# Norm and gate products of expert choice inside the last periods of logic attention; LSTM choices of 24 steps laid singly over steps 1 to 3

## The chip, the cores and the metric

The kernel runs on one core of one Trainium2 chip. Its engines are PE (TensorE), DVE (VectorE), ACT (ScalarE), POOL (GpSimd) and SP (SyncE, which here only issues DMAs). Each engine runs its own list of instructions in order; they meet at semaphores. The metric is the device time of one execution in microseconds, as the median of several runs. Of the kernel before, three runs were timed.

## The reference, cut to what matters

The input is a batch of 32 images and 32 texts. A token stage makes 36 tokens of 128 features from each image and appends 77 text rows, so `h` holds 32 blocks of 113 x 128. Four layers follow, each added to its input:

```python
h = h + _L0_attn_ref(_layernorm(h), ...)   # logic attention: 8 heads, two score maps, a small convolution of six maps
h = h + _L0_ffn_ref(_layernorm(h), ...)    # expert choice: 8 experts each choose their 28 best rows of an image
h = h + _L1_attn_ref(_layernorm(h), ...)   # attention with relative places
h = h + _L1_ffn_ref(_layernorm(h), ...)    # 8 LSTM experts, 2 chosen for each row
```

Expert choice starts from the softmax of `x @ Wg` over the 8 experts, `x` being the layernormed rows. The last layer takes the 32 images as 32 time steps of 113 rows. For each row the two largest of 8 router logits are chosen (ties go to the lower expert) and weighted by a softmax of the two. Each of the 16 pairs (choice, expert) runs an LSTM over the steps on the rows masked with that choice:

```python
i_, f_, g_, o_ = split(xt @ Wi + h @ Wh + b)
c = sigmoid(f_) * c + sigmoid(i_) * tanh(g_)
h = sigmoid(o_) * tanh(c)
y = h @ Wo + bo
```

The output is the sum over the 16 pairs of mask times weight times `y`.

## The kernel before, in words

`build` keeps `h` (113 rows x 32 images x 128) and `hT` (128 x 32 x 113, the normed rows turned) in SBUF and calls four stages, each a `Phase` with its own tiles and semaphores that closes with a barrier of all engines. Inside a phase each `block()` closes with a barrier too.

**Logic attention** (`logic_attention`, lines 396 to 997) is a software pipeline over periods p = -4 to 33. In period p, image p goes through the convolution and its gates, image p-1 (m) has its scores mixed and raised to the exponential, image p-2 (e) is turned, attended, projected out and added to `h`, and images p+2 to p+4 (f, z) are prepared. The order is written out by hand for each engine. ACT switches between two tables of functions in every period (lines 809 and 822): one holds the gelu, the other the logarithm and the exponential. From period 30 on stages drop out: period 32 has only the mixing of image 31 and the output of image 30, period 33 only the output of image 31. In period 32 DVE does the mixing of image 31 before it copies the turned weights of image 30 (line 920); ACT raises the mix (763) between them.

**Expert choice** (`expert_choice`, from line 1000) has three blocks. The first only issues six DMAs on SP: the gate weights and five constants, w1 and w2 of 1 MB and b2 of 0.5 MB among them (lines 1018 to 1023). The second is `norm_and_turn` (lines 112 to 200), in four groups of eight images: DVE takes the row statistics, ACT the root, ACT and DVE scale the rows into `hn`, PE turns four images into one PSUM bank, ACT moves the bank to `hT`, and PE makes the gate products of the bank's images. The third block is the stage itself. Its DVE part makes the softmax of the gates. Its PE part begins with

```python
pe.wait_ge(consts_in, 80)
pe.wait_ge(s["gate_ready"], 1)
```

where 80 is all five constants, and then turns the gates (line 1100) for the choice of the 28 best rows.

**LSTM experts** (`lstm_experts`, from line 1583) runs the same norm for its router logits and then one block. Step t has 8 experts, n = 8t+e, and four pairs of experts, q = 4t+p. PE makes for each n four gates: three passes of the input (line 1749) and, from step 1, three of the state (1757), since float32 values are split into a high and a low float16 part. After expert 3 of step t it makes the output product of step t-1 (`outputs`, 1711) with the bias row (1712). ACT takes four gates per n (1794), the tanh of the cell (1801) and the high part of the state (1805). DVE's round q is: state of q-1 (1878), masked inputs of step t+1 (1867), low part of the state (1893), weighing (1886), the sum over the two choices (1900), then the new cell of q (a product 1907 and a sum 1910). The PSUM ring lets PE be three n ahead of ACT.

The choices of steps 0 to 7 are made before the first step. The choices of the other three groups of 8 steps are made in steps 1, 2 and 3 (`choice`, 7 and 6 small DVE operations, and `weigh_choices`, 3). PE turns each group's masks and weights behind expert 1 of the next step, ACT copies them, and SP writes them to DRAM. From there `masks(t)` and `weights(t)` load a step's masks, weights and weight rows (1681) spread over 128 partitions. `hT` is split into high and low parts in groups of 2, 6, 8, 8 and 8 images (`PARTS_OF`). The weights of the recurrent product are split in step 0, a pair in each round.

## Time and profile before

| what | us |
|---|---|
| timed runs | 2380.01, 2381.17, 2381.90 |
| median | 2381.17 |
| the profiled execution, own time | 2382.08 |
| its span | 2380.3 |
| PE busy | 2126.8 (89%) |
| DVE busy | 1712.8 (72%) |
| ACT busy | 1664.8 (70%) |
| POOL busy | 334.2 (14%) |
| mean granted clock of PE | 0.932 |

The profile is that of one execution. A timeline row has the start in us from the span's start, the duration, the engine, the source line, the operation, what it writes and reads, and how many such instructions in a row were merged (x8). In brackets stands the idle time of that engine just before, and what ended it. A stage row has the length of the stretch, then for PE, its weight loads (PEld), DVE, ACT and POOL the busy time and the instructions, then the granted clock (1.00 is 2.4 GHz, 0.50 is 1.2 GHz), the share of the DMA engines and GB/s. Busy time is summed over a stretch, and idle time of an engine that is not the bound costs nothing.

### The profile page before, as it was taken

Reading aid. Unit: us, or ns where it says so; the run is one execution under the profiler, and the core shown is the slowest. Engines: PE = TensorE matmul, PEld = TensorE weight load, DVE = VectorE, ACT = ScalarE, POOL = GpSimd, SP = SyncE. Lnnn points to the kernel's source line nnn. Section 1 sums busy time; section 2 is a strip of 40 time slices with the busy share of each in tenths; the row PEclk is TensorE's granted clock in tenths of the full one; section 3 lists DMA queues with packets and bytes.
Section 4 is the critical chain, followed back from the end, with each engine's and each line's share of the span. In section 5 each row is a group of like instructions: output and inputs, shape, how many; then the busy total and the mean of one; then the engine's idle time right before and its main releaser. Section 6 shows DMA issues by size and latency. Waiting matters only on the chain. (4 is left out here: it accounts for less than half of the span.)

```text
span 2380.3 us, 55433 instructions
## 1 busy us (share of the span) xinstructions
PE 2126.8 (89%) x22214; PEld 1520.6 (64%) x22214; DVE 1712.8 (72%) x2729; ACT 1664.8 (70%) x3075; POOL 334.2 (14%) x198
## 2 busy tenths in 40 slices
PE   6699999999999999998549799987789999999998
PEld 3554444544444444443137588846689999999997
DVE  4457888888888888886554344535898888888887
ACT  3478888888888888888523336732667777777776
POOL 0122222222222222221000013410000000000000
PEclk9589999999999999999759869997799999999998
DMA  6288888888888888888110000001212222122220
GB/s 181 69 246 225 235 230 221 227 227 228 234 227 220 230 225 233 230 228 202 45 45 1 10 2 2 2 24 72 83 61 69 75 75 70 65 72 70 75 75 21
DMA packets 113273, 305.20 MB, mean 128 GB/s; under 512 B 20559, under 2 KB 57545, under 8 KB 112506
## 3 DMA queue, kind: packets, MB, share of 16 engines
q1 hardware_dynamic: 113018, 301.66, 45.0%
q8 instruction: 177, 2.90, 0.5%
q14 instruction: 78, 0.64, 0.1%
HBM read 168.64 MB, written 80.65 MB: 105 GB/s over the span
## 5 line engine op out<-in xcount | busy, mean ns | idle before, releaser
L746 ACT ACTIVATE la_hid<-ps,la_b 128x904 f32<-128x904 f32 (+1 forms) x480 | 451.0, 991 | 105.1 <-PE ps L598 104.4
L1749 PE MATMUL ps<-ls_xm,ls_w_in_parts 128*128 128x226 f16 x3072 | 471.7, 263 | 10.5 <-DVE ls_xm L1867 5.2
L1757 PE MATMUL ps<-ls_state_parts,ls_w_rec_parts 128*128 128x226 f16 x2976 | 450.3, 260 | 0.0
L1794 ACT ACTIVATE ls_gates<-ps,ls_bias 128x226 f32<-128x226 f32 x768 | 299.3, 444 | 62.4 <-PE ps L1757 61.9
L1749 PEld LDWEIGHTS ps<-ls_xm,ls_w_in_parts 128*128 128x128 f16 x3072 | 296.6, 98 | 21.6 <-DVE ls_xm L1867 5.6
L598 PE MATMUL ps<-la_pairs,la_w 32*64 32x452 f32 x3584 | 294.0, 569 | 12.1 <-ACT la_hid L746 12.0
L1757 PEld LDWEIGHTS ps<-ls_state_parts,ls_w_rec_parts 128*128 128x128 f16 x2976 | 286.3, 96 | 7.1
L611 PE MATMUL ps<-la_hid,la_w 128*32 128x452 f32 x1856 | 242.3, 559 | 15.2 <-ACT la_opened L752 15.2
L566 POOL TENSOR_TENSOR la_P<-la_P,la_inv 113x904 f32<-113x904 f32 x64 | 107.6, 1703 | 573.8 <-DVE la_soft L896 560.6
L611 PEld LDWEIGHTS ps<-la_hid,la_w 128*32 128x32 f32 x1856 | 42.1, 108 | 195.6 <-issue 95.6
L752 ACT ACTIVATE la_opened<-ps,la_b 128x904 f32<-128x904 f32 x128 | 129.8, 1014 | 43.8 <-PE ps L611 37.5
L1801 ACT ACTIVATE ls_tc<-ls_cells 128x452 f32<-128x452 f32 x128 | 74.3, 581 | 107.9 <-DVE ls_cells L1910 106.0
L633 PEld LDWEIGHTS ps<-la_k,la_q 32*113 32x113 f32 x1024 | 64.8, 184 | 127.7 <-DVE la_S L849 57.6
L1907 DVE TENSOR_TENSOR ls_prod<-ls_gates,ls_cells 128x904 f32<-128x904 f32 x128 | 139.9, 1093 | 0.0
L849 DVE COPY la_S<-ps 113x904 f32<-113x904 f32 x64 | 70.2, 1096 | 96.5 <-PE ps L633 96.5
L598 PEld LDWEIGHTS ps<-la_pairs,la_w 32*64 32x64 f32 x3584 | 77.8, 131 | 92.8 <-ACT la_hid L746 39.1
L1878 DVE TENSOR_TENSOR ls_state<-ls_gates,ls_tc 128x452 f32<-128x452 f32 x128 | 80.5, 629 | 71.1 <-ACT ls_tc L1801 70.8
L633 PEld LDWEIGHTS ps<-la_q,la_k 32*113 32x113 f32 x1024 | 65.7, 184 | 94.2 <-issue 45.0
L633 PE MATMUL ps<-la_k,la_q 32*113 32x113 f32 x1024 | 88.8, 293 | 37.0 <-DVE la_S L849 33.5
L572 POOL TENSOR_TENSOR la_P<-la_S,la_top 113x904 f32<-113x904 f32 x64 | 108.5, 1695 | 80.7 <-DVE la_top L852 80.7
L1794 ACT ACTIVATE ls_cells<-ps,ls_bias 128x226 f32<-128x226 f32 x256 | 116.2, 454 | 0.0
L1489 ACT ACTIVATE hT<-ps,ra_top 113x113 f32<-113x113 f32 x256 | 86.7, 366 | 39.3 <-DVE ra_top L1515 39.3
(293 smaller groups left out, 4072.4 us busy)
## 6 DMA issues: line engine op xcount, KB each, us to landing
la_pairs<-la_maps SPq DMA_DIRECT2D x224, 452.0 KB, 6.5
la_gate<-la_opened SPq DMA_DIRECT2D x448, 113.0 KB, 3.5
ls_w_all<-ls_weights SPq DMA_DIRECT2D x32, 904.0 KB, 4.1
la_maps<-la_ST SPq DMA_DIRECT2D x32, 791.0 KB
la_maps<-la_S SPq DMA_DIRECT2D x32, 791.0 KB
ls_m_all<-ls_masks SPq DMA_DIRECT2D x31, 456.0 KB, 3.7
la_maps<-la_Cr SPq DMA_DIRECT2D x32, 395.5 KB
la_maps<-la_Cl SPq DMA_DIRECT2D x32, 395.5 KB
```

The costliest lines, as they stand in the source:

```text
L566: pool.tensor_tensor(x, x, per_head(inv[:, i * H:(i + 1) * H]), ALU.mult).then_inc(s["P_ready"], 1)
L572: pool.tensor_tensor(P[:, z % 2, i, :, 0:N], by_head(S[:, z % 4, i]), per_head(top[:, i]), ALU.subtract).then_inc(s["shifted"], 1)
L598: mm = pe.matmul(ps[64 * hf:64 * hf + 64, CA + i, 0:HALF], w1[rows].rearrange("p r o -> p (r o)"), left[:, c % 2, x] if g == G else pairs[ ...
L611: mm = pe.matmul(ps[32 * i:32 * i + 32, GA + g % 2, 0:HALF], w2[:].rearrange("p r c k -> p (r c k)"), hid[:, (2 * g + i // 2) % 4, i % 2, ...
L633: mm = pe.matmul(ps[0:N, X + bank, col(2 * t + part)], *(sides if i < 2 else sides[::-1]), start=True, stop=True)
L746: act.activation(hid[:, u % 4, 0:n], ps[:, bank:bank + n, 0:HALF], ACT.Gelu_apprx_tanh, bias=b1[:])\
L752: act.activation(opened[:, pair % 2], ps[:, GA:GA + 2, 0:HALF], ACT.Tanh, bias=b2[:], scale=0.5)\
L1489: a = act.activation(z[:, b % 4, place_of * N:(place_of + 1) * N], ps[0:N, 2 * (b % SETS) + bank, at:at + N], ACT.Exp, bias=top[:, b % 2, ...
L1749: mm = pe.matmul(out_j, w_in_parts[:, w, e, j, :], xm[:, t % 2, e, :, x, 0:N], start=((w, x) == PASSES[0]), stop=(t == 0 and (w, x) == PAS ...
L1757: mm = pe.matmul(out_j, w_rec_parts[:, w, e, j, :], state_parts[:, x, e], start=False, stop=((w, x) == PASSES[-1]))
L1794: return act.activation(dst, ps[:, n % 3 * 2 + j // 2, j % 2 * 256:j % 2 * 256 + C], ACT.Tanh if j == 3 else ACT.Sigmoid, bias=bias[:, e, ...
L1907: signal(dve, dve.tensor_tensor(prod[:], gates[:, q % 2, 0:2], cells[:, p], ALU.mult), s["products_ready"], q + 1)
```

## The change

The tile `P` of logic attention now lies in a buffer `room` that both stages share; its first 4096 columns later hold the normed rows, which expert choice reads as `hn`. Its DMA of the gate weights moves to the loads of the first stage, and its call of `norm_and_turn` goes. In its place logic attention has, on DVE, `row_statistics` and `row_variance` of images 0 to 27 in period 31, their `row_scale` at the head of period 32, the statistics of images 28 to 30 in period 33 and those of image 31, the variance and the scale after the loop. ACT takes the first root at the end of period 31, scales 16 rows and moves four banks in period 32 before the mix is raised, and does the rest after the loop. PE turns four banks and makes two banks' gate products in period 32, and the rest after the loop. `ln_variance` (five small operations) and `ln_scale` (two) are the helpers that the norm used before.

In the LSTM stage the choices of steps 8 to 31 are made together, one to three operations in a round from step 1 to step 3, each over 24 steps; PE turns them in step 4, and SP stores them in its step 6. `PARTS_OF` is 2 images and then 4 each (the last 2). The cell update of step 0 is one product, and the memset of the cells goes. The masked inputs of step 1 are made one pair in each round of step 0. In each round the weighing comes before the low part. The choice weights of steps 0 to 7 are made one pair later.

```diff
-        P, PT = sb("P", [N, 2, 2, H, PV]), sb("PT", [N, 2, W])
+        P, PT = room[:].rearrange("p (b i h n) -> p b i h n", b=2, i=2, h=H), sb("PT", [N, 2, W])
+        rows, ln = room[:, 0:B * D].rearrange("p (b d) -> p b d", b=B), ln_tiles(ph, "ln", N)
...
+                def turn_rows(k):
+                    pe.wait_ge(s["rows_ready"], k + 1)
...
+                    for i in range(4):
+                        tr = pe.transpose(ps[:, k, i * N:(i + 1) * N], rows[:, 4 * k + i, :], ident[0:N, 0:N])
+                    tr.then_inc(s["rows_turned"], 1)
+                def gate_rows(k):
+                    pe.wait_ge(s["rows_moved"], k + 1)
+                    for i in range(4):
+                        mm = pe.matmul(ps[0:N, k, 4 * N + 8 * i:4 * N + 8 * i + 8], hT[:, 4 * k + i, :], w_gate[:], start=True, stop=True)
+                    mm.then_inc(s["gated"], 1)
...
+                    if p == B:
+                        for four in range(4):
+                            turn_rows(four)
+                            if four >= 2:
+                                gate_rows(four - 2)
...
+                for four in range(4, 8):
+                    turn_rows(four)
+                    gate_rows(four - 2)
+                gate_rows(6)
+                gate_rows(7)
+                pe.wait_ge(s["gated"], 8)
...
+                def root(n, images):
+                    act.wait_ge(s["row_var"], n + 1)
+                    act.activation(ln["std"][:, images], ln["var"][:, images], ACT.Sqrt, bias=eps[0:N], scale=1.0 / D)\
...
+                def scale_rows(k):
+                    act.wait_ge(s["row_scale"], 1 if 4 * k < EARLY else 2)
...
+                    for b in range(4 * k, 4 * k + 4):
+                        a = act.activation(rows[:, b, :], h[:, b, :], ACT.Identity, bias=ln["offset"][:, b:b + 1],
+                                           scale=ln["rstd"][:, b:b + 1])
+                    a.then_inc(s["rows_ready"], 1)
+                def move_rows(k):
+                    act.wait_ge(s["rows_turned"], k + 1)
...
+                    if p == B:
+                        scale_rows(0)
+                        for k in range(4):
+                            if k < 3:
+                                scale_rows(k + 1)
+                            move_rows(k)
+                    if p <= B:
+                        act.preload_act_table_set("natural_log_exp_and_others")
...
-                    act.preload_act_table_set("gelu_apprx_tanh_and_others")
+                    if p < B - 1:
+                        act.preload_act_table_set("gelu_apprx_tanh_and_others")
+                    if p == B - 1:
+                        root(0, slice(0, EARLY))
+                for k in range(4, 7):
+                    scale_rows(k)
+                for k in range(4, 7):
+                    move_rows(k)
+                root(1, slice(EARLY, B))
+                scale_rows(7)
+                move_rows(7)
+                act.wait_ge(s["rows_moved"], 8)
...
+                def row_statistics(lo, hi):
+                    dve.wait_ge(s["added"], hi)
+                    for b in range(lo, hi):
+                        dve.bn_stats(ln["stats"][:, b, :], h[:, b, :]).then_inc(s["row_stats"], 1)
+                def row_variance(images):
+                    dve.wait_ge(s["row_stats"], images.stop)
+                    ln_variance(dve, steps, ln, images, s["row_var"])
+                def row_scale(n, images):
+                    dve.wait_ge(s["row_std"], n + 1)
+                    ln_scale(dve, steps, ln, images, s["row_scale"])
...
+                    if p == B:
+                        row_scale(0, slice(0, EARLY))
...
+                    if p == B - 1:
+                        row_statistics(0, EARLY)
+                        row_variance(slice(0, EARLY))
+                    if p == B + 1:
+                        row_statistics(EARLY, B - 1)
...
+                row_statistics(B - 1, B)
+                row_variance(slice(EARLY, B))
+                row_scale(1, slice(EARLY, B))
...
-        hn = sb("hn", [N, B, D])
-        w_gate = sb("w_gate", [D, E])
+        hn = room[:, 0:B * D].rearrange("p (b d) -> p b d", b=B)
...
-                sp.dma_start(w_gate[:], dram["ec_w_gate"]).then_inc(gate_in, 16)
...
-        norm_and_turn(nc, "ec_norm", h, hT, ps, ident, eps, hn, w_gate, gate_in, 16)
...
-    M, SPREAD = 8, (2, 4, 5, 7)
-    PARTS_OF = ((0, 2), (2, 8), (8, 16), (16, 24), (24, 32))
+    FIRST, SPREAD = 8, (2, 4, 5, 7)
+    PARTS_OF = ((0, 2),) + tuple((lo, min(lo + 4, T)) for lo in range(2, T, 4))
...
-                    if 3 <= t <= 5:
-                        store(t - 2)
+                    if t == 6:
+                        store(1)
...
                 def turn_weights(g):
                     pe.wait_ge(s["wmasks_ready"], g + 1)
-                    turn(g, 256, wmask, s["w_turned"])
+                    if g:
+                        pe.wait_ge(s["m_ready"], 2)
+                    turn(g, 0 if g else 256, wmask, s["w_turned"])
...
-                        if 2 <= t <= 4 and e == 1:
-                            turn_masks(t - 1)
-                            turn_weights(t - 1)
+                        if t == 4 and e == 1:
+                            turn_masks(1)
+                        if t == 4 and e == 5:
+                            turn_weights(1)
...
-                        if side == 0 and q >= P:
-                            act.wait_ge(s["products_ready"], q - P + 1)
+                        if side == 0 and P <= q < 2 * P:
+                            act.wait_ge(s["cell_ready"], q - P + 1)
+                        elif side == 0 and q >= P:
+                            act.wait_ge(s["products_ready"], q - 2 * P + 1)
...
+                    if p == 2 and t + 1 < len(PARTS_OF):
                         hT_high(t + 1)
-                    if 1 <= t <= 3 and p == 2:
-                        second(t)
-                    if 2 <= t <= 4 and p == 1:
-                        masks_out(t - 1)
-                        weights_out(t - 1)
+                    if t == 3 and p == 2:
+                        second(1)
+                    if t == 4 and p == 1:
+                        masks_out(1)
+                    if t == 4 and p == 3:
+                        weights_out(1)
...
+                    if q < P:
+                        dve.tensor_tensor(cells[:, p, 1], gates[:, q % 2, 0], cells[:, p, 0], ALU.mult).then_inc(s["cell_ready"], 1)
+                        return
+                    signal(dve, dve.tensor_tensor(prod[:], gates[:, q % 2, 0:2], cells[:, p], ALU.mult), s["products_ready"], q - P + 1)
...
+                def largest(g, k):
...
                     steps.done(dve.tensor_reduce(top, logit[:, at], AX_X, ALU.max))
-                    steps.done(dve.tensor_tensor(pick[:, at], logit[:, at], top.unsqueeze(2).broadcast_to(wide), ALU.is_equal))
-                    steps.done(dve.tensor_tensor(pick[:, at], pick[:, at], order[:].unsqueeze(1).broadcast_to(wide), ALU.mult))
+                    steps.done(dve.tensor_tensor(pick[:, at], logit[:, at], wide(top, at), ALU.is_equal))
+                def first_of(g):
...
+                    steps.done(dve.tensor_tensor(pick[:, at], pick[:, at], order[:].unsqueeze(1).broadcast_to([N, at.stop - at.start, E]),
+                                                 ALU.mult))
                     steps.done(dve.tensor_reduce(late[:, at], pick[:, at], AX_X, ALU.max))
-                    picked = dve.tensor_tensor(chosen, pick[:, at], late[:, at].unsqueeze(2).broadcast_to(wide), ALU.is_equal)
+                def chosen(g, k):
...
+                    picked = dve.tensor_tensor(mask[:, at, :, k], pick[:, at], wide(late[:, at], at), ALU.is_equal)
...
-                        steps.done(dve.tensor_scalar(pick[:, at], chosen, -1e38, None, ALU.mult))
+                        steps.done(dve.tensor_scalar(pick[:, at], mask[:, at, :, k], -1e38, None, ALU.mult))
...
                 spread_inputs(0)
-                weigh_choices(0)
                 w_in_low(1)
                 spread_inputs(1)
+                weigh_choices(0)
...
                 w_in_low(3)
-                signal(dve, dve.memset(cells[:, :, 1], 0.0), s["zero_set"], 3)
...
                     if q:
+                        weigh(q - 1)
                         low_part(q - 1)
-                        weigh(q - 1)
                         choose(q - 1)
                     new_cell(q)
                     if t == 0:
+                        mask_inputs(1, p)
                         w_rec_low(p)
-                        if p >= 2:
-                            mask_inputs(1, 2 * p - 4)
-                            mask_inputs(1, 2 * p - 3)
-                        if p == 3:
-                            hT_low(1)
-                    if 1 <= t <= 3:
-                        if p == 0:
-                            choice(t, 0)
-                        if p == 1:
-                            choice(t, 1)
-                            hT_low(t + 1)
-                        if p == 3:
-                            weigh_choices(t)
+                    if p == 3 and t + 1 < len(PARTS_OF):
+                        hT_low(t + 1)
+                    if t == 1 and p == 0:
+                        largest(1, 0)
+                    if t == 1 and p == 2:
+                        first_of(1)
+                    if t == 2 and p == 0:
+                        chosen(1, 0)
+                    if t == 2 and p == 2:
+                        largest(1, 1)
+                    if t == 3 and p == 0:
+                        first_of(1)
+                    if t == 3 and p == 1:
+                        chosen(1, 1)
+                    if t == 3 and p == 3:
+                        weigh_choices(1)
                     if q % P == 3 and q >= P:
                         add_outputs(q // P - 1)
```

## Rows read from the trace of the kernel before

**Rows 1.** Stages: busy us of each engine (instructions), granted clock, DMA share, GB/s.
```profile
1210.00:1220.00 10.00, 10.00 (x52) 9.11 (x52) 3.22 (x16) 6.75 (x17) 0.00 (x0) 0.50 0.00 0
...
1840.00:1860.00 20.00, 20.00 (x203) 19.46 (x201) 16.76 (x29) 15.17 (x39) 0.00 (x0) 1.00 0.23 75
```

**Rows 2.** Timeline of ACT, drain and norm: start, us, line, operation, idle before.
```profile
1165.52 1.28 ACT L809 ACT_TABLE_LOAD   x1
...
1166.81 0.96 ACT L763 ACTIVATE la_mix<-la_mix 113x904 f32<-113x904 f32 x1
...
1183.93 0.96 ACT L763 ACTIVATE la_mix<-la_mix 113x904 f32<-113x904 f32 x1 [11.64 <-DVE la_mix L890]
...
1203.18 2.42 ACT L192 ACTIVATE ec_hn<-h,ec_norm_ln_offset,ec_norm_ln_rstd 113x128 f32<-113x128 f32 x6 [0.59 <-DVE ec_norm_ln_offset L103]
...
1206.51 0.55 ACT L198 ACTIVATE hT<-ps 128x452 f32<-128x452 f32 x1 [0.22 <-PE ps L171]
```

**Rows 3.** Timeline of DVE over the same stretch.
```profile
1167.80 1.09 DVE L913 TENSOR_REDUCE la_mix_total<-la_mix 113x8 f32<-113x904 f32 x1 [13.31 <-ACT la_mix L763]
...
1195.19 0.29 DVE L950 TENSOR_TENSOR h<-ps,h 113x128 f32<-113x128 f32 x1 [0.86 <-PE ps L703]
...
1199.84 1.64 DVE L134 BATCH_NORM_STATS2 ec_norm_ln_stats<-h 113x6 f32<-113x128 f32 x8 [4.35 <-PEq L1015]
...
1226.39 0.15 DVE L1180 MEMSET ec_ones<- 128x113 f32 x1 [10.94 <-PEq L54]
```

**Rows 4.** Timeline of PE, norm and start of expert choice.
```profile
1210.30 0.99 PE L171 MATMUL ps<-ident,ec_hn 113*128 113x113 f32 x4
...
1211.08 1.55 PE L160 MATMUL ps<-ec_w_gate,hT 128*113 128x8 f32 x8
...
1231.43 0.61 PE L1100 MATMUL ps<-ident,ec_gate 113*128 113x113 f32 x2 [6.13 <-DVE ec_gate L1189]
```

**Rows 5.** Timeline of the DMA issues of SP.
```profile
1196.64 0.37 SPq L1018 DMA_DIRECT2D ec_w_gate<-in_ec_w_gate  x1
...
1683.32 0.43 SPq L1681 DMA_DIRECT2D ls_w_row<-ls_weights  x1
```

**Rows 6.** One microsecond of the norm, columns as in Rows 1.
```profile
1207.00:1208.00 1.00, 0.51 (x2) 0.31 (x2) 1.00 (x6) 1.00 (x4) 0.00 (x0) 0.50 0.07 29
```

**Rows 7.** Timeline of PE in the LSTM stage.
```profile
1701.27 0.75 PE L1749 MATMUL ps<-ls_xm,ls_w_in_parts 128*128 128x226 f16 x3 [5.23 <-DVE ls_xm L1867]
...
1712.93 1.91 PE L1711 MATMUL ps<-ls_w_out,ls_hc 128*113 128x128 f32 x16
...
1732.71 0.32 PE L1715 MATMUL ps<-ident,ls_wmask 113*128 113x113 f32 x1 [3.22 <-DVE ls_wmask L1939]
...
1786.68 1.91 PE L1711 MATMUL ps<-ls_w_out,ls_hc 128*113 128x128 f32 x16
...
1807.65 1.91 PE L1711 MATMUL ps<-ls_w_out,ls_hc 128*113 128x128 f32 x16
...
2372.84 3.76 PE L1711 MATMUL ps<-ls_w_out,ls_hc 128*113 128x128 f32 x16 [8.02 <-DVE ls_hc L1900]
```

**Rows 8.** Timeline of DVE in the LSTM stage.
```profile
1685.00 1.56 DVE L1977 MEMSET ls_cells<- 128x1808 f32 x1 [0.33 <-issue]
...
1686.60 1.10 DVE L1907 TENSOR_TENSOR ls_prod<-ls_gates,ls_cells 128x904 f32<-128x904 f32 x1
...
1709.25 0.63 DVE L1878 TENSOR_TENSOR ls_state<-ls_gates,ls_tc 128x452 f32<-128x452 f32 x1
...
1713.72 0.21 DVE L1921 TENSOR_REDUCE ls_best<-ls_logit 113x8 f32<-113x64 f32 x1
...
1810.67 0.63 DVE L1893 TENSOR_TENSOR ls_state_parts<-ls_state,ls_state_parts 128x452 f16<-128x452 f32 x1
...
2366.66 0.63 DVE L1893 TENSOR_TENSOR ls_state_parts<-ls_state,ls_state_parts 128x452 f16<-128x452 f32 x1 [0.65 <-ACT ls_state_parts L1805]
```

**Rows 9.** One DMA issue: KB, us from issue to landing.
```profile
ls_w_row<-ls_weights SPq DMA_DIRECT2D x1, 7.1 KB, 6.1
```

More of the change, by code:

```diff
@@ L454, in logic_attention @@
         PERIODS = range(-4, B + 2)
+        EARLY = B - 4
         def ok(b):
@@ L1963, in _ @@
                 signal(dve, dve.memset(turned_m[:, :, N:NP], 0.0), s["zero_set"], 1)
-                choice(0, 0)
-                choice(0, 1)
+                for k in range(K):
+                    largest(0, k)
+                    first_of(0)
+                    chosen(0, k)
                 signal(dve, dve.memset(hT_parts[:, :, :, N:NP], 0.0), s["zero_set"], 2)
```

71 lines of the change are left out of this document (46 added, 25 removed).

## The prediction, made blind

> **What bounds the kernel now.** The profiled execution took 2382.08 us, its span 2380.3 us; the median of the three timed runs is 2381.17 us. I read the table of stages first, then the timelines of each engine over the two stretches that the diff touches, then the DMA issues. In the steady LSTM steps the reader sees PE busy 20.00 of 20 us at the full granted clock [rows 1]: PE sets the pace, one step in 1807.65 - 1786.68 = 20.97 us [rows 7], and nothing that DVE, ACT or SP saves in those steps counts. PE is not the bound in three places. First, from the last addition of logic attention, which ends at 1195.19 + 0.29 = 1195.48, to the first instruction of expert choice's main block at 1226.39 [rows 3]: 30.9 us of barrier, DMA issues, norm, turning and gate products, every engine partly idle, PE at half the clock even where it is busy 10.00 of 10 us [rows 1]. Second, LSTM steps 0 to 4: PE waits 5.23 us for the masked inputs before step 1, and 3.22 us for the first turned choice weights [rows 7]. Third, the very end: PE has idled 8.02 us before the last output product [rows 7], so the last step is closed by the DVE/ACT chain, not by PE.
>
> **Part 1, the norm in the drain.** Removed: the norm block of expert choice with its exit. Added: the same 32 rows, turns and gate products, 16 rows inside the last periods and 16 after them.
> (a) The statistics of 28 images come in period 31 after DVE's absolute value. Eight take 1.64 us, so 28 take 5.7 us, and the variance about 0.9; DVE has 13.31 us idle there [rows 3]. Cost nothing; without that cover it would be 6.6 us.
> (b) In period 32 the scale for 28 images stands ahead of DVE's mixing, which is the path there: two small operations. Rows 2 show 0.59 us from root to first scaled row, so 0.3 to 0.6; I take 0.4.
> (c) In the same period ACT scales 16 rows (six in 2.42 us, so 6.4 us) and moves four banks (0.55 each, 2.2 us) [rows 2] and loads the exponential table, 1.28. DVE's mixing, ten operations of about 1.1 us that end at 1183.9, began at 1173.0, so the scaling starts near 1173.4 and the table is in near 1184.3. The next exponential started at 1183.93 after 11.64 us of idle [rows 2] and is now 0.4 later: just covered, 0 to 1 us exposed, I take 0. The four turns and two gate products on PE lie in the wait for DVE's copy.
> (d) After the last period PE does turn 4, gate 2, turn 5, gate 3, turn 6, in that order. A turn of four is 0.78 us start to start (1211.08 - 1210.30), a gate product at most 1.55 [rows 4]; I use 0.8 and 1.5. That is 5.4 us from 1195.5. ACT is queued behind turn 6: move 0.55, table of the square root 1.28 [rows 2], root about 0.3, then 0.59 to the scaled row, four rows 1.6 us: 1205.3. Turn 7, gates 5, 6 and 7 are 0.8 + 4.5: logic attention ends at 1210.7 instead of 1195.48. DVE's work for the last image (under 2 us after the addition) is hidden behind PE's turns.
> Row and page differ on the table: an activation starts at 1166.81 right behind a load that started at 1165.52, so a switch costs 1.3 us here [rows 2]. The Trainium skill (ScalarE: Activation LUTs, What ACT_TABLE_LOAD costs) gives 1283 ns for the load and about 1380 ns more for a drain. By the page this part would be 1.4 us dearer; the row decides.
> (e) The exit is 1196.64 - 1195.48 = 1.16 us [rows 3, 5]: SP starts loading the weights at 1211.8. DVE started 3.20 us after SP's first issue [rows 3, 5]; one issue (0.4) is gone, so DVE starts at 1214.6, and the softmaxed gates are ready 1231.43 - 1226.39 = 5.0 later [rows 3, 4], at 1219.7. But PE may not turn them before all five constant loads have landed. Before, the norm hid them; their traffic dies out between 1207 and 1208 [rows 6], 10.6 to 11.4 us after SP's start. Now nothing hides them: less 0.4 for the issue gone, plus up to 1.4 for the completion, they land at 1222.0 to 1224.2; I take 1222.8. The turn that stood at 1231.43 moves to 1222.8: **gain 8.6 us** (without the wait 11.7; with a late landing and an exposed (c) 6).
>
> **Part 2, LSTM step 0.** The memset of the cells (1.56 us after 0.33 idle) goes: 1.9. The cell update of the first four pairs was a product of 904 columns (1.10) and an addition (0.63); now it is one operation of 452 columns (0.63): 1.1 each, 4.4 for four [rows 8]. The masked inputs of step 1 come one pair per round instead of two in the third and fourth; PE waited for just those [rows 7]. New on the path: the weighing stands ahead of the low part, so in round 0 everything on DVE queues behind it (low part, hidden sum, next cell, the low recurrent weights), and it waits for the row of weights, whose DMA was issued at 1683.32 and took 6.1 us to land [rows 5, 9]: 1689.4, and about 0.3 later as the choice weights are made later. DVE asks for it near 1688.7. That takes 0.4 to 1.5 back; I take 0.8. 1.9 + 4.4 - 0.8 = **5.5 us**. The bounds are 2 (if ACT's gates, which turned out between DVE's operations, set the round) and 7.
>
> **Part 3, steps 1 to 4.** From the first output product (1712.93) to that of step 4 (1786.68) there are 73.75 us, where three steady steps are 62.9: 10.8 us of waits, of slow clock after them, and of the turns [rows 7]. Of before, three sets of choices of 8 steps (13 small DVE operations of 0.21 us and 3 for the weights, each set, [rows 8]) sat in steps 1 to 3, and PE waited for each set's weights at the second expert of the next step. Now each operation does 24 steps at once: between 0.21 (fixed cost alone) and 0.63 (all of it per column); I take 0.35. Two lie in one round, and DVE's idle in a round (0.65 waiting for ACT's tanh, as the same wait in rows 8) takes 0.7. Only the mask with its -1e38 step (three operations) and the weights (three, with a low part of 4 images) go beyond it, about 0.4 and 0.9 us; the rounds become 0.1 shorter by the order weigh, low, choose, since the sum no longer follows its operand directly. I expect these to vanish. PE asks for the turned masks in step 4, one step after they are made. SP stores them in its step 6 and needs them in step 8: hidden. PE's turns are six as before, but all in step 4 and not yet in the count above: 1.3 us to pay (6 x 0.2, near the 0.32 of rows 7). **10.8 - 1.3 = 9.5 us**; bounds 4 (two thirds of the DVE excess stays) and 10.8.
>
> **Part 4, steady steps and end.** The low part now comes 0.6 us later. PE needs it a step later (below). The wait of the low part for ACT, 0.65 us [rows 8], is covered by the weighing. In the steady steps that is worth nothing, PE being full. In the last step, without masked inputs, each round waits 0.65; three rounds are 1.9 us, and the last gates cap it: **1.5 us**, bounds 0 and 2.6.
>
> **Sum.** 8.6 + 5.5 + 9.5 + 1.5 = 25.1 us. 2382.08 - 25.1 = 2357.0 for a profiled execution; the median lies 0.9 below it: 2356.
>
> **Rivals.**
> A. The early LSTM steps stay bound by DVE. For it: DVE is busy 16.76 of 20 even in steady steps [rows 1], and the 24-step operations could cost 0.63 each; the start could be ACT's. Against it: DVE loses 10 us of work and waits in these steps. Price: step 0 gives 2 and steps 1 to 4 give 4, so 8.6 + 2 + 4 + 1.5 = 16.1: 2365.
> B. The drain gives more: the weights land early or the gates do not wait, 11.7 for part 1, and parts 2 and 3 at their upper bounds: 11.7 + 7 + 10.8 + 1.5 = 31: 2350.
> C. PE's clock. The table shows 0.50, the 1.2 GHz level, through a stretch in which PE was busy 10.00 of 10 us [rows 1]. If the turns and gate products after the drain ran at 2.4 GHz, because the attention products come right before them, half of the 5.4 + 0.8 + 4.5 us of turns and gates on the path would go: about 5 us more, 2351. Against it is that row. The Trainium skill (TensorE: Matmul & The Clock Gate, Part 1) says that sustained work brings the array to 2.4 GHz; by that rule 2351, and this trace disagrees in the very instructions that move.
> D. Slower than before: the low part, moved behind the weighing, comes too late for PE's recurrent products. It would cost 0.66 us in each of 124 rounds, 82 us: 2438. It decides from the point where a pair's low part ends less than 0.66 before PE wants it. That of step 5's first pair ends at 1810.67 + 0.63 = 1811.3 [rows 8]; its use in step 6 is four experts ahead of the output product at 1807.65 + 20.97 = 1828.6, at about 2.4 us an expert 1819: 7.7 us of room.
> E. The change does not do what it says: part 1's tail grows as much as the norm costs (the weights' landing at 1231 and later) and step 0 only trades waits: within 0.2% of before, 2379.
>
> **How the numbers follow.** Forecast 0.66, A 0.15, B 0.08, C 0.06, D 0.02, E 0.03. What a measurement of this kernel can tell from no change is about 0.2%, 4.8 us. Cases of one sign hold nearly all, so the range goes from B and C to just below A: 2349 to 2365. Faster 0.95, same 0.03, slower 0.02.
>
> **What would show it.** In the trace after: no norm block of expert choice; the last gate product of logic attention near 1211; PE's turn of the gates waiting about 3 us for DMA, near 1223; ACT's mixing exponential of period 32 no later than 1185. In the LSTM, 5 to 6 us less to the first output product, counted from the block's start, then steps of 21 to 21.5 us with no wait for choice weights and the clock at 1.00; the last wait of PE near 6.5 us. The forecast is wrong if PE still waits for DVE in steps 1 to 3, if ACT's scaled rows delay the mixing by more than 1 us, or if a DMA wait in round 0 exceeds 2 us.

## The result, and the profile after

The changed kernel takes 2353.24 us (median of four, 2352.32 to 2355.66), the one before 2381.01 (2380.01 to 2381.9): ratio 0.9879, 95% interval 0.9867 to 0.9891, 27.8 us less. The forecast was 2356.0 in 2349 to 2365. The profiled execution has a span of 2350.5 us where the one before has 2380.3, 29.8 less. One execution of the changed kernel, the profiled one of its repeat e9, took 2986.24 us at a mean granted clock of 0.636 and is left out of every other number here. Cut at events that both traces have (a stretch is named by its ends, so A to B is the drain of logic attention, C to D the LSTM's start with step 0, D to E its steps 1 to 3), the 29.8 us are:

| stretch | before | after | difference |
|---|---|---|---|
| start to A, DVE's reciprocal of period 31 in logic attention | 1168.93 | 1166.90 | -2.03 |
| A to B, PE's turn of the gates in expert choice | 62.50 | 53.32 | -9.18 |
| B to C, DVE's first copy in the LSTM's main block (the one-hot) | 439.91 | 439.97 | +0.06 |
| C to D, first output product of the LSTM | 41.59 | 34.31 | -7.28 |
| D to E, fourth output product | 73.75 | 63.29 | -10.46 |
| E to the seventh | 62.93 | 63.23 | +0.30 |
| seventh to the last output product | 523.23 | 522.06 | -1.17 |
| last output product to the end | 7.46 | 7.42 | -0.04 |

The drain first. DVE in the changed kernel (start, us, line, operation, idle before; answers to [rows 3]):
```profile
1152.80 5.51 DVE L1032 BATCH_NORM_STATS2 la_ln_stats<-h 113x6 f32<-113x128 f32 x28
...
1165.77 1.09 DVE L988 TENSOR_REDUCE la_mix_total<-la_mix 113x8 f32<-113x904 f32 x1 [6.54 <-ACT la_mix L801]
...
1170.96 0.32 DVE L102 RECIPROCAL la_ln_rstd<-la_ln_std 113x28 f32<-113x28 f32 x1
...
1171.41 1.09 DVE L917 SCALAR_TENSOR_TENSOR la_soft<-la_diff,la_soft 113x904 f32<-113x904 f32 x1
...
1193.63 0.29 DVE L1025 TENSOR_TENSOR h<-ps,h 113x128 f32<-113x128 f32 x1 [0.86 <-PE ps L709]
```
The 28 statistics fill what was idle: 13.31 us have become 6.54. The scale costs 1171.41 - 1170.96 = 0.45 ahead of the mixing. (The answers to the recorded rows are the matching lines of the trace after.) ACT over the same stretch (answers to [rows 2]):
```profile
1180.55 1.28 ACT L873 ACT_TABLE_LOAD   x1
1182.37 0.96 ACT L801 ACTIVATE la_mix<-la_mix 113x904 f32<-113x904 f32 x1 [0.54 <-DVE la_mix L965]
...
1198.77 0.55 ACT L849 ACTIVATE hT<-ps 128x452 f32<-128x452 f32 x1 [1.65 <-PE ps L723]
1199.33 1.28 ACT L835 ACT_TABLE_LOAD   x1
1200.63 0.30 ACT L835 ACTIVATE la_ln_std<-la_ln_var,eps 113x4 f32<-113x4 f32 x1
1201.37 1.65 ACT L843 ACTIVATE weights_or_rows<-h,la_ln_offset,la_ln_rstd 113x128 f32<-113x128 f32 x4 [0.44 <-DVE la_ln_offset L103]
```
The exponential of the mixing still waits for DVE, so the scaled rows, moves and table cost nothing there. After the last addition the table of the square root stands behind the third move, and PE waits for it (PE, answers to [rows 4]):
```profile
1198.52 1.55 PE L729 MATMUL ps<-la_w_gate,hT 128*113 128x8 f32 x8
1203.07 1.02 PE L723 MATMUL ps<-ident,weights_or_rows 113*128 113x113 f32 x4 [2.99 <-ACT weights_or_rows L843]
1203.88 4.59 PE L729 MATMUL ps<-la_w_gate,hT 128*113 128x8 f32 x24
1220.22 0.64 PE L1196 MATMUL ps<-ident,ec_gate 113*128 113x113 f32 x2 [11.76 <-DMA ec_b<-in_ec_b]
```
The last wait names the constant loads. The gates had been ready since 1217.64 + 0.43 = 1218.07: 2.15 us of the 11.76 belong to the loads (DVE, and SP's first issue; the latter answers to [rows 5]):
```profile
1217.64 0.43 DVE L1285 TENSOR_TENSOR ec_gate<-ec_gate,ec_inv 113x256 f32<-113x256 f32 x1
```
```profile
1209.94 0.24 SPq L1117 DMA_DIRECT2D ec_place_no<-in_ec_place_no  x1
```
In the LSTM the output products come a steady step apart from the first on (21.03, 20.99, 21.27 and 21.27 us, the last two with three turns each), and the last wait is shorter (PE, answers to [rows 7]):
```profile
1694.50 1.97 PE L1811 MATMUL ps<-ls_w_out,ls_hc 128*113 128x128 f32 x16 [0.80 <-DVE ls_hc L2011]
...
1715.53 1.91 PE L1811 MATMUL ps<-ls_w_out,ls_hc 128*113 128x128 f32 x16
...
1757.79 1.91 PE L1811 MATMUL ps<-ls_w_out,ls_hc 128*113 128x128 f32 x16
...
1779.06 1.91 PE L1811 MATMUL ps<-ls_w_out,ls_hc 128*113 128x128 f32 x16
...
2343.08 3.76 PE L1811 MATMUL ps<-ls_w_out,ls_hc 128*113 128x128 f32 x16 [6.84 <-DVE ls_hc L2011]
```

### The profile page after: what moved, and what is told of

Its sections match the earlier page's. It is cut to its first block and busy times, and to the rows that moved or that the text cites. A ratio compares the mean times of both kernels' runs of the same rounds, so it can differ in the third digit from the quotient of the medians.

```text
span 2350.5 us, 55362 instructions
## 1 busy us (share of the span) xinstructions
PE 2118.8 (90%) x22214; PEld 1516.5 (65%) x22214; DVE 1678.8 (71%) x2674; ACT 1667.2 (71%) x3076; POOL 334.2 (14%) x198
## 5 line engine op out<-in xcount | busy, mean ns | idle before, releaser
L572 POOL TENSOR_TENSOR weights_or_rows<-weights_or_rows,la_inv 113x904 f32<-113x904 f32 x64 | 107.6, 1702 | 573.1 <-DVE la_soft L971 560.7
L578 POOL TENSOR_TENSOR weights_or_rows<-la_S,la_top 113x904 f32<-113x904 f32 x64 | 108.5, 1695 | 80.0 <-DVE la_top L927 80.0
L639 PE MATMUL ps<-la_q,la_k 32*113 32x113 f32 x1024 | 87.8, 290 | 19.9 <-DVE la_ych L912 10.6
```

The lines of the kernel that those rows point to most:

```text
L572: pool.tensor_tensor(x, x, per_head(inv[:, i * H:(i + 1) * H]), ALU.mult).then_inc(s["P_ready"], 1)
L578: pool.tensor_tensor(P[:, z % 2, i, :, 0:N], by_head(S[:, z % 4, i]), per_head(top[:, i]), ALU.subtract).then_inc(s["shifted"], 1)
L639: mm = pe.matmul(ps[0:N, X + bank, col(2 * t + part)], *(sides if i < 2 else sides[::-1]), start=True, stop=True)
```

## The experiments

Times are medians with their ratio to the kernel before and its 95% interval. Single executions of one kernel differed by up to 14 us (e4: 2354.28 to 2368.23), a lower granted clock going with the longer time (e2: 2364.15 at 0.937, 2375.97 at 0.930). So what is smaller than 2 to 3 us is decided by the stretches A to E of the profiled executions. Where kernels have the same instructions in a stretch, A to B repeats within 0.5 us (52.97 to 53.41 in six traces), C to D within 0.8 (34.31 to 35.10 in seven, mean 34.67), D to E within 0.01 (six); B to C, in which only e5, e10 and e11 move a wait, is 439.8 to 440.5 in ten of twelve traces, 442.6 in e10 and 447.9 in e6.

**Taking the change apart: e1 to e4.**

e1, the LSTM block of the kernel before under the changed drain.

> The changed kernel with the LSTM block of the kernel before; only the norm and the gate products of expert choice have moved into logic attention. Theory: the drain gives what the two traces show between the last addition of logic attention and the turn of the gates, 9.2 us, so 2371.8; the 2.0 us by which the changed kernel's trace is ahead before the drain is variation between profiled executions. Rival: those 2.0 us belong to the change (the shared room, the one more load), 2369.8, and the trace stands at about 1171 us, not 1173, at DVE's scale of period 32.

Measured 2373.5, 0.9968 (0.9956 to 0.998). A to B is 53.13, C to D 40.95, D to E 74.01. The drain is worth 9.4 in its stretch; B to C, C to D and D to E differ from the kernel before by +0.6, -0.6 and +0.3. A stands at 1169.54, later than in the kernel before: the 2.03 us ahead of the drain are not of the change. Over all twelve traces A lies between 1164.95 and 1169.54. Theory right, rival refuted.

e2, e1 with the edits on step 0:
```
-  signal(dve, dve.memset(cells[:, :, 1], 0.0), s["zero_set"], 3)
+  if q < P:
+      dve.tensor_tensor(cells[:, p, 1], gates[:, q % 2, 0], cells[:, p, 0], ALU.mult).then_inc(s["cell_ready"], 1)
+      return
...
-  if p >= 2:
-      mask_inputs(1, 2 * p - 4)
-      mask_inputs(1, 2 * p - 3)
+  mask_inputs(1, p)
```


> e1 and, of the LSTM edits, only those on step 0: no memset, one product for the cell, the masked inputs of step 1 one pair per round, the first weights of the choices after the second spread. Low part still ahead of the weighing, choices in sets of 8. Theory: 6.5 us less than e1, 2365.3; step 0 gives 5.5 to 7.3 by itself. Rival (as rival A of the prediction: ACT's gates set the rounds of step 0, and the gain came with the new order of weighing and low part): at most 3 us less than e1, 2368.8 or more.

Measured 2368.49, 0.9948 (0.9933 to 0.9964); C to D 35.68, 5.3 less than e1 and 5.9 less than before, D to E 73.98. The stretch is just under the theory's 5.5 and puts the rival (at most 3) out. The medians alone would not: they are 5.0 apart, and e2's executions run from 2364.15 to 2375.97.

e3, e2 with the weighing ahead of the low part, so the changed kernel with sets of 8:
```
   if q:
+      weigh(q - 1)
       low_part(q - 1)
-      weigh(q - 1)
       choose(q - 1)
```


> The changed kernel with the choices in sets of 8 steps as before, so e2 with the weighing ahead of the low part. Theory: the choices of 24 steps are worth 10.2 us, so 2363.4, and 1.5 to 2 us less than e2 (1.2 at the end, the rest in the early rounds); PE again waits for choice weights in steps 1 to 4. Rival: it was the order of weighing and low part that freed steps 1 to 4, and sets of 8 cost nothing then: 2353 to 2356.

Measured 2360.96, 0.991 (0.9898 to 0.9923); profiled execution 7.1 us under e2's (own times 2358.80 and 2365.94). C to D 34.94, **D to E 69.31**, last step 1.18 less, and 0.64 less from the last output product to the end, which is variation (6.76 in e3, 7.40 to 7.46 in all others). Both expectations failed: the theory had left less than 1 us to the order in the early rounds, and it takes 4.7 of the 10.5 us of D to E by itself; the rival had put the sets at nothing, and they cost 6.0.

e4, the changed kernel with the low part first again (the diff above turned round).

> The changed kernel with the low part ahead of the weighing, as before. Theory: only the last step loses, 1.2 us, and up to 1 in step 0: 2354.5 to 2355.5, with the last wait of PE near 8.0 us; steady steps the same 20.97 to 21.0. Rival: the order carries the early steps too, 2357 or more. Second rival (the low part comes too late in the changed kernel, rival D of the prediction in small): it gets faster, below 2353.

Measured 2356.53, 0.9904 (0.9886 to 0.9922); profiled own time 2355.30. C to D 35.60, D to E 63.95, last wait of PE 8.02 and the last step 1.17 longer. So beside sets of 24 the order is worth 0.7 in D to E, beside sets of 8 4.7: **the two edits are not a sum.** PE's waits in D to E show the state between (us in total, times, longest), e2 first, then e3:
```profile
PE ps L1811 <- DVE ls_wmask L2040: 6.3, 3, 3.3
PE ps L1807 <- DVE ls_hc L1998: 2.0, 1, 2.0
```
```profile
PE ps L1811 <- DVE ls_wmask L2040: 3.5, 2, 2.6
PE ps L1807 <- DVE ls_hc L1998: 1.0, 1, 1.0
```
Why the order matters is in DVE's rounds. One of e2, from the state to the first operation that is free to move, and one of the changed kernel:
```profile
1711.91 0.63 DVE L1976 TENSOR_TENSOR ls_state<-ls_gates,ls_tc 128x452 f32<-128x452 f32 x1 [0.65 <-ACT ls_tc L1897]
1712.46 0.63 DVE L1965 TENSOR_TENSOR ls_xm<-ls_hT_parts,ls_m_all 128x912 f16<-128x912 f16 x1
1713.19 0.63 DVE L1991 TENSOR_TENSOR ls_state_parts<-ls_state,ls_state_parts 128x452 f16<-128x452 f32 x1
1713.73 0.62 DVE L1984 TENSOR_TENSOR ls_wh<-ls_state,ls_w_all 128x452 f32<-128x452 f32 x1
1714.39 0.40 DVE L1998 TENSOR_TENSOR ls_hc<-ls_wh 128x226 f32<-128x226 f32 x1
...
1716.38 0.16 DVE L2038 TENSOR_SCALAR ls_weight<-ls_weight 113x8 f32<-113x8 f32 x1
```
```profile
1701.61 0.63 DVE L1989 TENSOR_TENSOR ls_state<-ls_gates,ls_tc 128x452 f32<-128x452 f32 x1 [0.65 <-ACT ls_tc L1911]
1702.15 0.63 DVE L1978 TENSOR_TENSOR ls_xm<-ls_hT_parts,ls_m_all 128x912 f16<-128x912 f16 x1
1702.70 0.62 DVE L1997 TENSOR_TENSOR ls_wh<-ls_state,ls_w_all 128x452 f32<-128x452 f32 x1
1703.24 0.62 DVE L2004 TENSOR_TENSOR ls_state_parts<-ls_state,ls_state_parts 128x452 f16<-128x452 f32 x1
1703.78 0.39 DVE L2011 TENSOR_TENSOR ls_hc<-ls_wh 128x226 f32<-128x226 f32 x1
...
1705.76 0.35 DVE L2043 TENSOR_TENSOR ls_pick<-ls_pick,ls_order 113x192 f32<-113x192 f32 x1
```
The same seven operations take 4.47 us before and 4.15 after. Of the 0.32, 0.12 is that the sum (`ls_hc`) no longer directly follows the product that it reads: it starts 0.66 us behind it in e2, and in the changed kernel each of these operations starts 0.54 or 0.55 behind the one ahead. The larger part, 0.18, is at the low part (`ls_state_parts`): right behind the masked inputs it starts 0.73 after them, at 1713.19, and ACT's high part of the same state ends at 1712.57 + 0.58 = 1713.15. No wait is named there, so that it is ACT's end that it waits for is read from these times; in step 0 of e2, where no masked inputs stand between, the same wait is named and is 0.65. The weighing fills it.

PE's round is 20.98 / 4 = 5.24. The room for other work is 0.77 a round before and 1.09 after, 9.3 and 13.1 us over the twelve rounds of steps 1 to 3. An estimate of what has to fit: 48 operations of sets of 8 at about 0.25 start to start, three additions of 0.28 and three low parts of 1.09 make 16 us; 16 operations of sets of 24 at 0.38 with three additions and three low parts of 0.55 make 8.6. 16 us fit in neither, 8.6 in both: 6.7 us stand out in e2 and 2.9 in e3. The excess over three steady steps (62.93) was 11.1, 6.4, 1.0 and 0.4 us in e2, e3, e4 and the changed kernel, so the estimate gives the difference of e2 and e3 (3.8 for 4.7) and leaves some 4 us of each. Most of that is PE itself, slower after its waits: in the first of the three steps of e2 the mean granted clock was 0.88 and PE was busy 24.47 us, in e3 0.93 and 22.93, in the changed kernel 1.00 and 21.03.

e8, whole choices of 24 steps in one round:
```
-  if t == 1 and p == 0:
-      largest(1, 0)
   ...
+  if 1 <= t <= 2 and p == 0:
+      largest(1, t - 1)
+      first_of(1)
+      chosen(1, t - 1)
```


> The changed kernel with the choices of 24 steps, but a whole choice (seven operations for the first, six for the second) in the first round of step 1 and of step 2, not one or two operations a round. Theory: a round with seven operations of 0.35 us is 1.7 us over what DVE has idle, and the stretch of the first four output products gets 1 to 3 us longer than 63.3: 2354.5 to 2356. Rival: only the number of operations counts, PE has its low parts well ahead: 2353.2, stretch 63.3.

Measured 2355.24, 0.9894 (0.9879 to 0.9909). D to E is 63.82, 0.5 more: closer to the rival. A round that is some 1.6 us too long (seven operations at 0.38 less the 1.09 of room) is made good by its neighbours. What counted is how much DVE has to do in steps 1 to 3, much less how it is laid.

**The waits left in the drain: e5, e6.**

e5:
```
-  pe.wait_ge(consts_in, 80)     (ahead of the turn of the gates)
+  pe.wait_ge(consts_in, 80)     (PE, ahead of the first hidden product)
+  dve.wait_ge(consts_in, 80)    (ahead of the first one-hot)
```


> The changed kernel, but PE waits for the five constant loads of expert choice only ahead of its first hidden product and DVE ahead of its first one-hot, instead of PE ahead of the turn of the gates. Theory: that wait is the last one in the drain and costs 2.15 us (gates ready 1218.07, turned 1220.22): the turn comes 2.1 us earlier after DVE's start, 51.2 us instead of 53.3 after the reciprocal of logic attention's period 31, and the time is 2351.1. Rival: the loads land later than the next user wants them, so the wait only moves to the one-hot: 2353.

Measured 2352.93, 0.9875 (0.9862 to 0.9889). A to B is 50.78, 2.5 less, and PE's turn now waits for DVE's gates:
```profile
1219.45 0.64 PE L1195 MATMUL ps<-ident,ec_gate 113*128 113x113 f32 x2 [9.22 <-DVE ec_gate L1285]
```
So the loads were the last wait there. Nothing is given back up to C (B to C 440.14). The time hardly shows it (the median is the rival's 2353), as A came at 1168.67 in this execution, 1.8 later than in the changed kernel's; the time proves nothing by itself.

e6:
```
-  for k in range(4, 7):
-      move_rows(k)
+  move_rows(4)
   root(1, slice(EARLY, B))
   scale_rows(7)
-  move_rows(7)
+  for k in range(5, 8):
+      move_rows(k)
```


> The changed kernel, but ACT computes the last square root and scales the last four rows right after its first move after the last period, not after its third. Theory: the 2.99 us that PE waits before its last turn of rows go, logic attention ends near 1205.4 on the scale of the changed kernel's trace instead of 1208.5; as everything behind moves along (SP's loads too), 3.0 us: 2350.2. Rival: the moves of ACT come late then, since 1.28 us of table and 1.65 of rows stand ahead of them, and PE waits for those instead: 1 us or less, 2352.5.

Measured 2347.56, 0.9869 (0.9849 to 0.9888), A to B 50.16: 3.2 less, as expected. PE has no wait between its turns any more:
```profile
1201.82 0.99 PE L723 MATMUL ps<-ident,weights_or_rows 113*128 113x113 f32 x4
1202.61 4.59 PE L729 MATMUL ps<-la_w_gate,hT 128*113 128x8 f32 x24
```
The median gains more than the stretch, and the profiled execution (2359.36) loses: in it the granted clock was 0.50 from 1400 to 1440, where the changed kernel's is 0.82 over the last 20 us, and B to C took 447.88 instead of 439.97. Such shifts of the clock inside relative attention are a noise that all times here share.

**PE's clock: e7.**
```
-  for i in range(4):                  (turn_rows: now turns 0 and 1 are made twice)
-      tr = pe.transpose(ps[:, k, i * N:(i + 1) * N], rows[:, 4 * k + i, :], ident[0:N, 0:N])
+  for i in range(8 if k < 2 else 4):
+      tr = pe.transpose(ps[:, k, i % 4 * N:(i % 4 + 1) * N], rows[:, 4 * k + i % 4, :], ident[0:N, 0:N])
   ...
+  def again(k, times):
+      pe.wait_ge(s["rows_moved"], k + 1)
+      for i in range(4 * times):
+          pe.transpose(ps[:, k, i % 4 * N:(i % 4 + 1) * N], rows[:, 4 * k + i % 4, :], ident[0:N, 0:N])
   ...
+  again(2, 5)    (period B, ahead of left_product and base)
+  again(2, 1)    (period B + 1, same place)
+  again(2, 3)    (ahead of turn_rows(7))
```


> The changed kernel with repeated turns of rows (same rows to the same places) put into PE's idle times after the last periods: the turns 0 and 1 twice, five more turns of four before the products of period 32's left side, one before the last mixing, three before the last turn; PE is then busy nearly all of 1173 to 1208. Theory: the granted clock stays at 0.50 as in the trace, where PE was busy without a gap too, and the time is 2353 to 2355 (each repeated turn that is late costs up to 0.8). Rival C of the prediction: the clock goes to 1.00 and the turns and gate products at the end take half of their time, 4 to 5 us less, 2349.

Measured 2350.70, 0.9865 (0.9852 to 0.9879), A to B 50.17. My theory was wrong. The stretches (busy us of each engine, granted clock, DMA share, GB/s):
```profile
1180.00:1182.00 2.00, 2.00 (x13) 2.00 (x12) 0.98 (x2) 1.90 (x4) 0.00 (x0) 0.50 0.00 0
1182.00:1184.00 2.00, 1.87 (x17) 1.52 (x19) 1.68 (x3) 2.00 (x7) 1.18 (x1) 0.50 0.00 0
1184.00:1186.00 2.00, 1.16 (x20) 0.84 (x13) 0.67 (x2) 1.99 (x6) 0.51 (x1) 0.89 0.00 0
1186.00:1188.00 2.00, 1.16 (x12) 0.94 (x10) 1.95 (x5) 0.00 (x0) 0.00 (x0) 1.00 0.00 0
...
1190.00:1192.00 2.00, 2.00 (x20) 2.00 (x19) 1.22 (x7) 0.90 (x2) 0.00 (x0) 0.82 0.00 0
1192.00:1194.00 2.00, 2.00 (x12) 2.00 (x13) 0.00 (x0) 0.36 (x2) 0.00 (x0) 0.50 0.00 0
```
After PE had turned rows and made gate products with hardly a gap since 1171.29 (44 single turns and 16 gate products up to 1183.64) the clock went from 1.2 to 2.4 GHz. From the reciprocal of the scale to the last addition it took 21.01 us instead of 22.67, and from there to the end of logic attention 13.22 instead of 14.55. The clock fell again after a stretch in which PE was busy 1.1 to 1.2 of each 2 us, while it was busy 2.00 of 2. The last 24 gate products took 4.59 as ever. The Trainium skill (TensorE: Matmul & The Clock Gate, Part 1) has it that sustained work brings the array to 2.4 GHz. The rise in e7 agrees with it; the kernel before does not: there PE was busy 17.80 of the 17.80 us from 1207.50 to 1225.30 (24 turns and 64 gate products), longer than in e7 before the rise, at 0.50 throughout. Which difference between the two decides is not shown.

**Together: e9 to e11.** e9 is the changed kernel on the chip of e10 and e11. (e1 to e4 ran on one chip, e5 to e8 on another, each with the kernel before beside them: 2382.29, 2382.07 and 2380.76 us on the three.)

> The changed kernel itself once more, for a reference on the chip on which e10 and e11 run, and for how much of a difference between profiled executions comes from the stretches that no edit touches. Theory: 2353 with single runs up to 2362 as in e2, e4, e6 and e8, 53.2 to 53.4 us again from the reciprocal of logic attention's period 31 to the turn of the gates, and a clock pattern between 1300 and 1450 us that moves from run to run. Rival: a chip's own speed makes the medians of e5 to e8: then also the first 1160 us differ by more than 3 us.

The three executions that count took 2352.87, 2353.04 and 2354.58 (ratio 0.9885, 0.987 to 0.99), as in the first comparison: no difference between chips is seen that could make the medians of e5 to e8. The profile is of the execution left out, so the expectation on its stretches and on the first 1160 us was not tested.

e10 has e5 and e6, and SP issues the five loads in the main block:
```
-  with ph.block() as block:      (a block of its own for the loads)
-      @block.sync
   with ph.block() as block:      (the main block of expert choice)
+      @block.sync                (the same five dma_start)
```


> The changed kernel with three edits in the drain: the square root first (e6), the wait for the loads later (e5), and the five loads issued by SP inside the main block of expert choice instead of a block of their own. Theory: the gains add up, since each takes a piece of one chain: 3.1 + 2.5 + 3.2 (SP's first issue to DVE's start), so 44.5 us from the reciprocal of period 31 to the turn of the gates instead of 53.3, and 8.8 less than the changed kernel: 2344.5. Rival: with the loads started only 6 us before the gates are turned, the first one-hot or hidden product waits for them, and 3 us of it come back: 2347.5.

**2345.25, 0.9849 (0.9836 to 0.9863), 7.8 us under e9's middle value.** A to B is 45.28 (44.5 expected), and no wait names a load:
```profile
PE ps L1199 <- DVE ec_rank L1303: 10.9, 2, 6.2
PE ps L1194 <- DVE ec_gate L1284: 6.9, 1, 6.9
PE ps L1148 <- DVE ec_hot L1252: 1.8, 1, 1.8
```
The gains add, but for 0.8: from the end of logic attention to DVE's first instruction behind it there are 1.93 us instead of 4.70, so the block that went was worth 2.8 and not 3.2. The rival had the loads give 3 us back behind B, and B to C was 2.6 longer here than in the changed kernel. It is not the loads: up to the first statistics of relative attention's norm it took 118.2 us from B, where the others have 117.9 to 118.7, and 442.6 came about behind that, where the clock at 200 to 220 us from B was 0.67 (0.78 to 0.83 in all others but e6, which has 0.50). The rival is refuted.

e11 adds to e10 the doubled turns and the calls of e7 without the last, more calls, and the table load:
```
-  again(2, 1)
+  again(2, 2)                                       (period B + 1)
+  again(2, 2)                                       (ahead of output(e), p >= B)
+  act.preload_act_table_set("sqrt_and_others")      (ahead of move_rows(4))
```


> e10 with the repeated turns of e7 (those ahead of the last turn not needed any more), two more groups of them ahead of each of the last two output products and one more behind the last mixing turn, and the table of the square root loaded ahead of the first move. In e7 the granted clock rose to 1.00 near 1184 and fell to 0.50 near 1191, after a stretch in which PE was busy 1.1 to 1.2 of each 2 us. Theory: with those gaps filled it stays at 1.00 through the last turns and gate products, and 4 to 6 us more go than in e10: 2339.5, and under 41 us from the reciprocal to the turn of the gates. Rival: the fall in e7 was not for the gaps but comes after a time at 1.00 whatever PE does; then it falls near 1191 again and the gain over e10 is that of e7 and the table, 2 to 3 us: 2342.

A to B is 40.58, as the theory wanted, but the median is 2344.62 (2338.97 to 2347.43), 0.9848 (0.9834 to 0.9861), no better than e10's. The clock:
```profile
1192.00:1194.00 2.00, 1.51 (x17) 1.42 (x17) 0.10 (x1) 1.87 (x5) 0.00 (x0) 1.00 0.03 8
1194.00:1196.00 2.00, 2.00 (x15) 1.96 (x14) 0.00 (x0) 1.07 (x3) 0.00 (x0) 0.64 0.00 0
1196.00:1198.00 2.00, 2.00 (x12) 2.00 (x12) 0.00 (x0) 0.00 (x0) 0.00 (x0) 0.50 0.00 0
```
It held some 3 us longer than in e7 and then fell in the middle of the gate products, with PE busy nearly all the time, so those 24 still took 4.47. Each explanation has half of it: the filled gaps helped, and the fall came all the same. What lets it fall was not tried. Two of the five executions are faster than any of e10 (the profiled one, 2338.97 at a clock of 0.942, and 2341.15 at 0.941), the other three are not (2344.62, 2345.04 and 2347.43 at 0.937 and 0.938). The profiled one is 6.9 under e10's, of which 4.7 are the stretch and 2.6 e10's long B to C; where the others lose the 4.7 is open.

## Why the prediction was right, point by point

1. **Part 1 (a) to (c), what the drain hides: right.** Idle 13.31 to 6.54; the scale 0.45 where 0.4 stood, though the sum then left this 0.4 out (8.6 should have been 8.2); nothing exposed at ACT's exponential, which still waits 0.54 for DVE.
2. **(d), the tail: right by 0.7.** From the end of the last addition (1193.92) to the end of logic attention (1208.47) it took 14.55; 15.2 had been added up. The first of the turns started at 1193.39, behind PE's output product and ahead of the addition's end, which the sum had as its start. The table cost 1.28 + 0.02 to the root; the 1.4 more that the Trainium skill (ScalarE: Activation LUTs, What ACT_TABLE_LOAD costs) gives for a drain did not appear in this trace. What the prediction passed over is that PE's wait of 2.99 for the last rows need not exist (e6).
3. **(e), the wait for the loads: right in kind, 0.9 too long.** 2.15 us beyond the gates, against about 3; gain of the part 9.2 (9.4 in e1) against 8.6, and e5 shows that the loads ended it. Inside it errors cancel. The exit took 1209.94 - 1208.47 = 1.47, not 1.16. DVE started 3.23 behind SP's first of five issues, as it had 3.20 behind the first of six, so the issue that went saved nothing. And the turn came 10.28 behind SP's first issue, where 11.0 had been taken: no row before showed the time of the loads' completion.
4. **Part 2, step 0: 7.3 in this trace, 6.9 by the mean of seven, against 5.5 with a bound of 7.** The memset, the single products and the masked inputs gave 5.3 to 5.9 (e2), near 1.9 + 4.4 = 6.3. The term that failed is the wait for the row of weights, -0.8. That wait was 0.27 at the weighing. Another one stood ahead of it that the prediction did not have, 1.02 for the masks of step 1 (0.81 in e2, which makes 5.5 of the 6.3):
```profile
1675.19 0.63 DVE L1978 TENSOR_TENSOR ls_xm<-ls_hT_parts,ls_m_all 128x912 f16<-128x912 f16 x1 [1.02 <-DMA ls_m_all<-ls_masks]
1677.77 0.63 DVE L1997 TENSOR_TENSOR ls_wh<-ls_state,ls_w_all 128x452 f32<-128x452 f32 x1 [0.27 <-DMA ls_w_row<-ls_weights]
```
   So the size of the -0.8 was met by luck. And the order, which the prediction had only as a cost, gave 0.7 to 0.9 on balance (e2 to e3; e4 against the mean), since the weighing fills DVE's wait for ACT's high part, which e2 has in three rounds of step 0:
```profile
1683.52 0.63 DVE L1991 TENSOR_TENSOR ls_state_parts<-ls_state,ls_state_parts 128x452 f16<-128x452 f32 x1 [0.65 <-ACT ls_state_parts L1901]
```
   The first part of the transposed rows, four images instead of six, was left out of the sum; what remains for it, 34.94 against 34.67, is within the spread.
5. **Part 3: the size right, 10.5 - 0.3 = 10.2 against 9.5, the reasoning half right.** Operations of 24 steps took 0.35 as assumed. The turns in step 4 cost 0.6 and not 1.3: three fall before E and three behind it, and the steps with them took 21.27 us each instead of 20.98. The order was put at 0.1 a round, which is what the sum no longer following its product gives (0.12), but it is worth 0.32: the low part's wait for ACT, which part 4 counted in the last step alone, is shorter in every round. And the argument counted what stands out of single rounds, where the total over twelve rounds decides (e3, e4, e8).
6. **Part 4: 1.17 against 1.5,** steady steps 20.98 as before. Last wait 6.84 against "near 6.5".
7. **Rivals.** A and E are out by the traces, D by e4 (low first gains nothing). B was half of it: parts 2 and 3 came near their upper bounds, part 1 did not. C was false for the changed kernel (0.50 throughout the tail), but its row did not settle it for good: in e7 and e11 the first of those instructions do run at the high clock (eight gate products in 0.87 us instead of 1.55), the last 24 gate products hardly or not at all.

So 25.1 + 0.6 (drain) + 1.8 (step 0) + 0.7 (choices and turns) - 0.3 (end) makes 27.8 before rounding, which the medians show and the two traces too (29.8 less 2.03 ahead of A). The mechanisms of the drain and of the sets of 24 were right; that the total came within 2.8 us rests in part on errors that cancel (3, 4 and 5).

## What to carry to other kernels

When a second engine limits a stretch, add up all that it has to do there against the pace of the first over the whole stretch; an order of two operations and a number of small operations then draw on the same room, and their gains do not add. When work is moved into a drain, look once more at what the old place had hidden: here a table load and a wait for weights became the path, and putting the root first, waiting for the loads only where they are used and starting them in the block that uses them (e10) gave another 7.8 us. A gain in one stretch shows in the time only if the clock's pattern behind it stays, so read the stretches as well as the medians.

## What was not expected of the hardware

The granted clock did not rise in 17.8 us of unbroken gate products and turns in the kernel before ([rows 1] show 10 of them), rose in e7 and e11 near 1184 after turns and gate products since 1171, and fell in e11 near 1195 in the midst of gate products with PE busy 2.00 of 2 us. Executions of one kernel differ by up to 14 us on the same chip (e4), with granted clocks from 0.930 to 0.938; the traces differ most inside relative attention, 200 to 220 us behind B (granted clock 0.50 in e6, 0.67 in e10, 0.78 to 0.83 in the others), where no edit reaches.
